# 8-dim attention heads: values and softmax denominators from one set of products, in a four-layer decoder on one core

## The chip, the cores and the metric

The program runs on one core of a Trainium2 chip. The metric is device time in microseconds of that core, lower is better. A core has five engines that run side by side, each with its own queue: PE (matrix products), DVE (vector work), ACT (pointwise functions), POOL (general vector work) and SP (which only starts transfers here). They are coupled by semaphores alone: an engine takes its instructions strictly in order and stops at a wait until another engine has signalled.

## The reference

A decoder of 32 sequences of 128 tokens, 128 features, passes through many layers. Four of them are attentions with 16 heads of 8 dimensions. All have this core (`_L0_attn_ref`):

```python
q = split_heads(x @ Wq + bq)          # 16 heads of 8
k = split_heads(x @ Wk + bk)
v = split_heads(x @ Wv + bv)
energy = jnp.einsum('bhqd,bhkd->bhqk', q, k)
energy = energy + bias[None]                              # L0_attn alone
att = jax.nn.softmax(energy / (scaling * temp), axis=-1)
out = jnp.einsum('bhqk,bhkd->bhqd', att, v)
out = out.transpose(0, 2, 1, 3).reshape(B, N, C)
return out @ Wp + bp
```

The second (the attention in `L1_ffn`) is causal, grouped in its keys and turned by rotary positions; the third (`L2_xattn`) takes keys and values from a context of 96 features and has a small two-layer projection behind it; the fourth (`L3_xattn`) takes keys and values from the context too. A residual and, but for the second, a layer norm follow.

## The kernel before

All four attentions are built by `attention8` (L682). It works on pairs of sequences: `n` counts the 32 sequences, `p = n // 2` the pairs, `s = n % 2` the half. The order of every engine is written out by hand in one loop over `n` per engine, and in it some steps stand only for even `n`, some only for odd ones.

For one sequence the softmax goes like this. PE forms rough scores of all heads in four PSUM banks (`score_roughly`, L1251, in two halves), DVE takes their row maxima (`maxima`, L1033, in two halves of 8 heads), PE turns the maxima (L1264), ACT copies them out (`evict_maxima`, L952), PE forms the exact scores with keys in the rows (L1271) and subtracts the maxima by a further product (L1279), and ACT takes the exponentials into `pT` (L966, L961 in `L0_attn`, again in two halves). Rough scores, exact scores and the next sequence's rough scores use the same four banks, so sequence after sequence goes through PE, DVE, PE and ACT in a ring. In `L0_attn` DVE adds the bias in between (`add_bias`, L1045), and there and in the causal layer PE adds bias or mask to the scores (L1233).

The rest hangs on the side of the ring. PE multiplies `pT` by the values, 16 products of 32 output rows each (`weigh`, L1293); `vz` holds the values with zeros around them so that the four heads of a 32-row group add up side by side. 16 further products by `ones4` sum `pT` over the keys, so that each of the 8 rows of a head holds its denominator (`add_up`, L1301). Both stand in one PSUM bank, `D`: columns 0 to 255 hold values of the pair, 256 to 511 denominators. In the trace every such product has two rows, so 16 of them read x32. When both sequences of pair `p-1` are in, DVE takes the reciprocal of the denominators (L1052) and multiplies (L1056) in `normalised(p-1)`, at even `n` behind the maxima; PE projects the result at odd `n` (`project_out`, L1324; with the hidden layer `hide`, L1312, and L1328), and DVE adds the residual (L1065).

```python
if n + 1 < NB:
    score_roughly(n + 1, [0])
if n >= 1:
    weigh(n - 1)
if n + 1 < NB:
    score_roughly(n + 1, [1])
if n >= 1:
    add_up(n - 1)
```

## Time and profile before

| | us |
|---|---|
| median of three runs | 3140.16 (3131.76 to 3142.49) |
| the profiled execution's own time | 3129.11 |
| its span, first to last instruction | 3127.3 |
| PE busy | 2682.1 (86%) |
| DVE busy | 1927.8 (62%) |
| ACT busy | 1380.7 (44%) |
| POOL busy | 1365.6 (44%) |

The stages run one after another. From the first to the last reading of rough scores (L1033) the four attentions stand at 16.5 to 247.3 us (`L0_attn`), 1255.6 to 1482.6 (`L1_ffn`), 1942.9 to 2148.6 (`L2_xattn`) and 2811.9 to 3001.1 (`L3_xattn`). Tile names in the profile leave the layer's number out: L_attn is `L0_attn` there, L_ffn the second, L_xattn the third and the fourth. A row of the timeline gives the start and the length of one or several merged instructions and, in brackets, how long the engine had stood idle before it and what ended that. PE durations run past the start of the next instruction, since products are pipelined; the time that one takes of the engine is the distance between starts.

### The profile page before, as it was taken

Reading aid. Unit: us, or ns where it says so; the run is one execution under the profiler, and the core shown is the slowest. Engines: PE = TensorE matmul, PEld = TensorE weight load, DVE = VectorE, ACT = ScalarE, POOL = GpSimd, SP = SyncE. Lnnn points to the kernel's source line nnn. Section 1 sums busy time; section 2 is a strip of 40 time slices with the busy share of each in tenths; the row PEclk is TensorE's granted clock in tenths of the full one; section 3 lists DMA queues with packets and bytes.
Section 4 is the critical chain, followed back from the end, with each engine's and each line's share of the span. In section 5 each row is a group of like instructions: output and inputs, shape, how many; then the busy total and the mean of one; then the engine's idle time right before and its main releaser. Section 6 shows DMA issues by size and latency. Waiting matters only on the chain. (4 is left out here: it accounts for less than half of the span.)

```text
span 3127.3 us, 78252 instructions
## 1 busy us (share of the span) xinstructions
PE 2682.1 (86%) x31745; PEld 1906.2 (61%) x31745; DVE 1927.8 (62%) x5040; ACT 1380.7 (44%) x3101; POOL 1365.6 (44%) x1474
## 2 busy tenths in 40 slices
PE   7894566666779997999999997998989999989986
PEld 4552333344446775565899985666367777765665
DVE  6888999355764444666544444564866666645665
ACT  4453555354445654444322223553144444435554
POOL 4773666173311222444233343553853333434556
PEclk9997777787889999999899997998999999999998
DMA  3000000400000001000000000001000000000000
GB/s 108 2 2 1 1 1 1 111 10 7 1 19 17 2 2 42 2 3 3 8 1 1 1 8 11 2 3 45 0 6 2 3 2 2 2 9 2 3 5 24
DMA packets 25796, 37.16 MB, mean 12 GB/s; under 512 B 760, under 2 KB 22656, under 8 KB 24576
## 3 DMA queue, kind: packets, MB, share of 16 engines
q1 hardware_dynamic: 25440, 32.16, 3.4%
q8 instruction: 255, 4.18, 0.6%
q14 instruction: 101, 0.83, 0.1%
HBM read 29.93 MB, written 2.23 MB: 10 GB/s over the span
## 5 line engine op out<-in xcount | busy, mean ns | idle before, releaser
L1501 POOL TENSOR_TENSOR L_attn__qk<-L_attn__turned 128x512 f32<-128x512 f32 x128 | 161.5, 1272 | 287.3 <-DVE L_attn__turned L1624 287.3
L4664 PE MATMUL psum<-L_ffn__e_hT,weights 128*128 128x256 f32 x1024 | 244.3, 382 | 0.0
L1033 DVE TENSOR_REDUCE L_xattn__nm<-psum 128x8 bf16<-128x1024 f32 x128 | 156.4, 1225 | 138.3 <-PE psum L1251 132.1
L1624 DVE TENSOR_TENSOR L_attn__turned<-psum,weights 128x1024 f32<-128x1024 f32 x128 | 153.4, 1219 | 94.0 <-PE psum L1737 89.2
L4664 PEld LDWEIGHTS psum<-L_ffn__e_hT,weights 128*128 128x128 f32 x1024 | 186.7, 192 | 20.2
L4511 DVE TENSOR_TENSOR L_ffn__e_a<-L_ffn__e_sg,psum 128x512 f32<-128x512 f32 x128 | 88.1, 688 | 176.0 <-ACT L_ffn__e_sg L4503 175.9
L4503 ACT ACTIVATE L_ffn__e_sg<-psum 128x512 f32<-128x512 f32 x128 | 76.4, 597 | 258.4 <-PE psum L4664 258.4
L966 ACT ACTIVATE L_xattn__pT<-psum 128x1024 f32<-128x1024 f32 x128 | 124.1, 1021 | 56.1 <-PE psum L1279 56.1
L1737 PE MATMUL psum<-L_attn__xT,weights 128*128 128x256 f32 x512 | 136.0, 399 | 3.9 <-DVE L_attn__turned L1624 3.2
L4677 PEld LDWEIGHTS psum<-weights,L_ffn__e_a 128*128 128x128 f32 x1024 | 134.4, 192 | 7.2 <-DVE L_ffn__e_a L4511 0.7
L4677 PE MATMUL psum<-weights,L_ffn__e_a 128*128 128x128 f32 x1024 | 135.1, 275 | 0.5 <-DVE L_ffn__e_a L4511 0.5
L4421 POOL TENSOR_TENSOR L_ffn__e_half<-L_ffn__e_prod 128x512 f32<-128x512 f32 x32 | 40.6, 1269 | 171.2 <-DVE L_ffn__e_prod L4520 171.2
L1552 ACT ACTIVATE L_attn__qk<-L_attn__qk 128x512 bf16<-128x512 f32 x128 | 77.2, 630 | 82.5 <-POOL L_attn__qk L1501 82.5
L1033 DVE TENSOR_REDUCE L_ffn__nm<-psum 128x8 bf16<-128x1024 f32 x64 | 78.2, 1225 | 55.4 <-PE psum L1251 55.4
L961 ACT ACTIVATE L_attn__pT<-L_attn__pT,L_attn__sc 128x1024 f32<-128x1024 f32 x64 | 73.0, 1149 | 76.3 <-DVE L_attn__pT L1045 76.3
L1737 PEld LDWEIGHTS psum<-L_attn__xT,weights 128*128 128x128 f32 x512 | 90.5, 192 | 25.6 <-issue 11.5
L3160 DVE MATCH_REPLACE8 L_xattn__front_left<-L_xattn__front_top,L_xattn__front_left 128x128 f32<-128x128 f32 x384 | 100.7, 273 | 0.0
L1033 DVE TENSOR_REDUCE L_attn__nm<-psum 128x8 bf16<-128x1024 f32 x64 | 78.0, 1221 | 24.8 <-PE psum L1251 24.8
L1633 DVE TENSOR_REDUCE L_attn__nm<-psum 128x8 bf16<-128x1024 f32 x64 | 75.4, 1220 | 26.4 <-PE psum L1770 25.8
L1972 POOL TENSOR_TENSOR L_xattn__rstd<-L_xattn__mv,eps 128x2 f32<-128x2 f32 x16 | 3.1, 195 | 198.3 <-DVE L_xattn__mv L2101 198.3
L1575 ACT ACTIVATE L_attn__pT<-psum 128x1024 f32<-128x1024 f32 x64 | 62.0, 1021 | 61.3 <-PE psum L1799 61.3
L3302 PE MATMUL psum<-L_xattn__front_diag,L_xattn__front_ex 128*128 128x128 f32 x256 | 53.5, 378 | 40.9 <-POOL L_xattn__front_ex L2989 39.4
(682 smaller groups left out, 7525.8 us busy)
## 6 DMA issues: line engine op xcount, KB each, us to landing
L_xattn__conv_toeplitz<-s4d_kernel SPq DMA_DIRECT2D x5, 1024.0 KB, 10.9
weights<-pack SPq DMA_DIRECT2D x1, 3328.0 KB, 12.6
weights<-pack SPq DMA_DIRECT2D x1, 3140.0 KB, 10.0
weights<-s4d_kernel SPq DMA_DIRECT2D x3, 1024.0 KB, 9.1
L_attn__bias_tables<-pack SPq DMA_DIRECT2D x1, 2048.0 KB, 9.9
out_dram<-X SPq DMA_DIRECT2D x8, 256.0 KB, 2.3
weights<-pack SPq DMA_DIRECT2D x1, 1603.5 KB, 15.0
ctxT<-ctxT_in SPq DMA_DIRECT2D x1, 1536.0 KB, 12.0
```

The source lines that it names most:

```text
L966: nc.scalar.activation(unit, scores[u], ACT.Exp, scale=scale).then_inc(p_sb, 1)
L1033: nc.vector.tensor_reduce(nm[:, n % 2, :].rearrange("p (g c) -> p g c", g=4)[:, 2 * u:2 * u + 2, 0:4], scores[u].rearrange("p g (i q) -> p ...
L1501: nc.gpsimd.tensor_tensor(qk[:, p % 2, u], turned[:, g % 2, :, 0:2 * P], turned[:, g % 2, :, 2 * P:4 * P], ALU.add).then_inc(qk_sb, 1)
L1552: nc.scalar.activation(qk16[:, p % 2, u], qk[:, p % 2, u], ACT.Copy).then_inc(qk16_sb, 1)
L1624: nc.vector.tensor_tensor(turned[:, g % 2], proj[u % 2].unsqueeze(1).to_broadcast([P, 2, 4 * P]), k.w(name + "rope").rearrange("p (t q) -> ...
L1633: nc.vector.tensor_reduce(nm[:, n % 2, :].rearrange("p (g c) -> p g c", g=4)[:, 2 * u:2 * u + 2, 0:4], scores[u].rearrange("p g (j q) -> p ...
L1737: last = nc.tensor.matmul(proj[place % 2][:, 2 * P * t:2 * P * t + 2 * P], w[:, P * c:P * c + P], xT[:, p % 2, :], start=True, stop=True)
L3160: last = nc.vector.match_replace(left[:, u % 2, j, h, :], top[:, u % 2, j, h, 8 * r:8 * r + 8], source(u, r, j, h), 2 * NEG)
L4503: nc.scalar.activation(sg[:, g % 2, :], gate[g % 2], ACT.Silu).then_inc(sg_sb, 1)
L4511: nc.vector.tensor_tensor(a[:, g % 2].rearrange("p c s q -> p (c s q)"), sg[:, g % 2, :], up[g % 2], ALU.mult).then_inc(a_sb, 1)
L4664: last = nc.tensor.matmul(bank[g % 2][:, 256 * c:256 * c + 256], k.w(name + w)[:, o:o + P], hT, start=True, stop=True)
L4677: last = nc.tensor.matmul(Y[s][e // 4][:, P * (e % 4):P * (e % 4) + P], a[:, g % 2, c, s, :], k.w(name + "Wd")[:, P * (2 * e + c):P * (2 * ...
```

## The change

The zeros of `vz` beside each head's values become ones in 8 columns. The weights of one product are then, for a head, 8 columns of values and 8 of ones (even heads) or ones and values (odd heads), with zeros in the other 16. One set of 16 products gives values and denominators: the bank `D` holds even heads in columns 0 to 255 and odd heads in columns 256 to 511, and in each the values of a head in its own 8 rows and its denominators in the 8 rows of its neighbour (or the other way round). `add_up` goes.

To get them in place, ACT scales the even-head half by two 0/1 masks (`own_half`: the values that stand right, and the denominators), DVE adds the odd-head half with the opposite masks (`both_halves`, two instructions), so `both[:, 0]` holds all values and `both[:, 1]` all denominators, the latter in their neighbour's rows. DVE takes the reciprocal of these, PE exchanges neighbouring groups of 8 rows by a permutation matrix (`swap`, two products of 128x128x128), and DVE multiplies (`normalised`). These steps are put at fixed places of each engine's loop, and PE's `project_v`, `project_out` and `weigh` change places with the rough scores.

```diff
-        vz = sb("vz", [P, 2, 2, 4, 4, 40])
+        vz = sb("vz", [P, 4, 4 * P + 2 * D8])
+        own, both = sb("own", [P, 2, 2 * P]), sb("both", [P, 2, 2 * P])
...
-                nc.gpsimd.memset(vz[:], 0.0).then_inc(zeroed, 1)
+                for kind in range(2):
+                    heads = vz[:, :, 2 * P * kind:2 * P * kind + 2 * P].rearrange("p a (m c) -> p a m c", c=4 * D8)
+                    nc.gpsimd.memset(heads[:, :, :, D8 - D8 * kind:2 * D8 - D8 * kind], 1.0)
+                    last = nc.gpsimd.memset(heads[:, :, :, 2 * D8:4 * D8], 0.0)
+                last.then_inc(zeroed, 1)
...
+                def own_half(p):
+                    act.wait_ge(pv_ps, 2 * p + 2)
...
+                    if p >= 1:
+                        act.wait_ge(both_sb, p)
+                    for kind in range(2):
+                        last = nc.scalar.activation(own[:, kind, :], D[:, 0:2 * P], ACT.Identity,
+                                                    scale=halves_of_16[:, kind:kind + 1])
+                    last.then_inc(own_sb, 1)
...
                         if p < LAST:
                             evict_v(p + 1)
+                        if p >= 1:
+                            own_half(p - 1)
...
+                def both_halves(p):
+                    dve.wait_ge(own_sb, p + 1)
...
+                    for kind in range(2):
+                        last = nc.vector.scalar_tensor_tensor(
+                            out=both[:, kind, :], in0=D[:, 2 * P:4 * P], scalar=halves_of_16[:, 1 - kind:2 - kind],
+                            in1=own[:, kind, :], op0=ALU.mult, op1=ALU.add)
+                    last.then_inc(both_sb, 1)
+                    dve.wait_ge(both_sb, p + 1)
+                    if p >= 1:
+                        dve.wait_ge(rd_ps, p)
+                    nc.vector.reciprocal(rd[:], both[:, 1, :]).then_inc(rd_sb, 1)
+
                 def normalised(p):
-                    dve.wait_ge(pv_ps, 2 * p + 2)
-                    nc.vector.reciprocal(rd[:], D[:, 2 * P:4 * P]).then_inc(rd_sb, 1)
-                    dve.wait_ge(rd_sb, p + 1)
+                    dve.wait_ge(rd_ps, p + 1)
                     if p >= 2:
                         dve.wait_ge((hid_ps if mlp else y_ps), p - 1)
-                    nc.vector.tensor_tensor(oT[:, p % 2, :], D[:, 0:2 * P], rd[:], ALU.mult).then_inc(o_sb, 1)
+                    nc.vector.tensor_tensor(oT[:, p % 2, :].rearrange("p (s q) -> p s q", s=2),
+                                            D[:].rearrange("p (s e q) -> p s e q", s=2, e=2)[:, :, 1, :],
+                                            both[:, 0, :].rearrange("p (s q) -> p s q", s=2),
+                                            ALU.mult).then_inc(o_sb, 1)
...
+                    if n % 2 == 1 and p >= 1:
+                        normalised(p - 1)
                     if n + 1 < NB:
                         maxima(n + 1)
...
                         if p >= 1:
-                            normalised(p - 1)
+                            both_halves(p - 1)
...
-                    if s == 0 and p >= 1:
-                        pe.wait_ge(o_sb, p)
...
+                    if p >= 1:
+                        pe.wait_ge(o_sb if s == 1 else both_sb, p)
+                    for kind in range(2):
+                        for i in range(2):
+                            for g in range(4):
+                                m = 2 * g + i
+                                o = 2 * P * kind + 4 * D8 * m - 2 * D8 * i
+                                last = nc.tensor.matmul(
+                                    D[32 * g:32 * g + 32, 2 * P * kind + P * s:2 * P * kind + P * s + P],
+                                    vz[:, p % 2 * 2 + s, o:o + 4 * D8], pT[:, n % 2, 2 * m + kind, :], start=i == 0,
+                                    stop=i == 1, skip_group_check=True)
                     last.then_inc(pv_ps, 1)
+
+                def swap(p):
+                    pe.wait_ge(rd_sb, p + 1)
+                    for s in range(2):
+                        last = nc.tensor.matmul(D[:, 2 * P * s + P:2 * P * s + 2 * P], k.w("swap8"),
+                                                rd[:, P * s:P * s + P], start=True, stop=True, skip_group_check=True)
+                    last.then_inc(rd_ps, 1)
...
                     score(n, turned)
+                    if n % 2 == 1 and p >= 1:
+                        swap(p - 1)
```

PE's queue, one odd `n` of `L3_xattn`, before (L1186 turns the next x, L1251 are rough scores, L1301 is `add_up`):

```order
L1279 MATMUL psum<-L_xattn__nmT,sel 128x128 x16
L1186 MATMUL psum<-const,X 128x128 x2
L1324 MATMUL psum<-weights,L_xattn__oT 128x128 x2
L1251 MATMUL psum<-L_xattn__k16m,L_xattn__q 128x512 x2
L1293 MATMUL psum<-L_xattn__pT,L_xattn__vz 32x128 x16
L1251 MATMUL psum<-L_xattn__k16m,L_xattn__q 128x512 x2
L1301 MATMUL psum<-L_xattn__pT,const 32x128 x16
L1264 MATMUL psum<-ident_bf,L_xattn__nm 64x128 x2
```

The same stretch of PE's queue in the changed kernel (L1348 is `swap`, L1295 rough scores, L1370 the projection, L1339 `weigh`):

```order
L1323 MATMUL psum<-L_xattn__nmT,sel 128x128 x16
L1348 MATMUL psum<-L_xattn__rd,const 128x128 x2
L1230 MATMUL psum<-const,X 128x128 x2
L1295 MATMUL psum<-L_xattn__k16m,L_xattn__q 128x512 x2
L1370 MATMUL psum<-weights,L_xattn__oT 128x128 x2
L1295 MATMUL psum<-L_xattn__k16m,L_xattn__q 128x512 x2
L1339 MATMUL psum<-L_xattn__pT,L_xattn__vz 32x128 x16
L1308 MATMUL psum<-ident_bf,L_xattn__nm 64x128 x2
```

The exchange stands directly behind the exact scores and ahead of both halves of the next rough scores; `add_up` is gone, and `weigh` stands behind the second half.

DVE's queue over one pair of `L3_xattn` before, beginning at even `n`:

```order
L1033 TENSOR_REDUCE L_xattn__nm<-psum 128x2x4 x2
L1052 RECIPROCAL L_xattn__rd<-psum 128x256
L1056 TENSOR_TENSOR L_xattn__oT<-psum,L_xattn__rd 128x256
L1033 TENSOR_REDUCE L_xattn__nm<-psum 128x2x4 x2
L1065 TENSOR_TENSOR L_xattn__res<-psum,L_xattn__xb 128x256
L1071 BN_STATS L_xattn__st<-L_xattn__res 128x6 x2
L1074 BN_AGGR L_xattn__mv<-L_xattn__st 128x2 x2
```

And in the changed kernel:

```order
L1056 TENSOR_REDUCE L_xattn__nm<-psum 128x2x4 x2
L1081 SCALAR_TENSOR_TENSOR L_xattn__both<-psum,const,L_xattn__own 128x256 x2
L1088 RECIPROCAL L_xattn__rd<-L_xattn__both 128x256
L1094 TENSOR_TENSOR L_xattn__oT<-psum,L_xattn__both 128x256
L1056 TENSOR_REDUCE L_xattn__nm<-psum 128x2x4 x2
L1106 TENSOR_TENSOR L_xattn__res<-psum,L_xattn__xb 128x256
L1112 BN_STATS L_xattn__st<-L_xattn__res 128x6 x2
L1115 BN_AGGR L_xattn__mv<-L_xattn__st 128x2 x2
```

Two instructions come ahead of the reciprocal, and the multiplication behind it now waits for PE's exchange before the next maxima can be taken.

## Rows read from the trace of the kernel before

**Rows 1.** Busy time by engine over the four attentions' stretches, summed

```profile
sum 884.00, PE 823.02 PEld 515.42 DVE 600.77 ACT 442.01 POOL 471.02; mean PE 205.76 PEld 128.86 DVE 150.19 ACT 110.50 POOL 117.75
```

**Rows 2.** Busy time of line L1301 (add_up) over the four stretches

```profile
sum 896.00, PE 141.12; mean PE 35.28
```

**Rows 3.** Timeline of PE in L3_xattn: start, length, what, idle before

```profile
2927.65 0.61 PE L1225 MATMUL psum<-weights,ctxT 96*128 96x128 f32 x4
2928.19 0.39 PE L1251 MATMUL psum<-L_xattn__k16m,L_xattn__q 32*128 32x512 bf16 x2
...
2929.84 1.08 PE L1301 MATMUL psum<-L_xattn__pT,const 128*32 128x128 f32 x32
2930.85 0.62 PE L1264 MATMUL psum<-ident_bf,L_xattn__nm 128*64 128x128 bf16 x2
...
2933.45 0.68 PE L1324 MATMUL psum<-weights,L_xattn__oT 128*128 128x128 f32 x4 [0.30 <-DVE L_xattn__oT L1056]
```

**Rows 4.** Timeline of ACT in L3_xattn

```profile
2920.89 1.94 ACT L966 ACTIVATE L_xattn__pT<-psum 128x1024 f32<-128x1024 f32 x2 [0.86 <-PE psum L1279]
...
2926.76 1.94 ACT L966 ACTIVATE L_xattn__pT<-psum 128x1024 f32<-128x1024 f32 x2 [1.01 <-PE psum L1279]
2928.59 0.48 ACT L917 ACTIVATE L_xattn__kT<-psum,weights 128x256 f32<-128x256 f32 x1
...
2931.05 0.45 ACT L933 ACTIVATE L_xattn__vz<-psum 128x128 f32<-128x128 f32 x2 [1.25 <-PE psum L1301]
...
2932.80 1.94 ACT L966 ACTIVATE L_xattn__pT<-psum 128x1024 f32<-128x1024 f32 x2 [0.86 <-PE psum L1279]
```

**Rows 5.** Timeline of DVE in L3_xattn

```profile
2928.62 2.56 DVE L1033 TENSOR_REDUCE L_xattn__nm<-psum 128x8 bf16<-128x1024 f32 x2 [2.40 <-PE psum L1251]
2931.09 1.75 DVE L1052 RECIPROCAL L_xattn__rd<-psum 128x256 f32<-128x256 f32 x1
2932.88 0.42 DVE L1056 TENSOR_TENSOR L_xattn__oT<-psum,L_xattn__rd 128x256 f32<-128x256 f32 x1
```

**Rows 6.** Groups by line and form: count, busy us, mean ns of one

```profile
L4003 DVE SCALAR_TENSOR_TENSOR L_ffn__npre<-psum,weights,L_ffn__rh 128x256 f32<-128x256 f32 x8 | 3.9, 484 | 0.3
L4013 DVE SCALAR_TENSOR_TENSOR L_ffn__hnew<-L_ffn__zd,L_ffn__nt 128x256 f32<-128x256 f32 x8 | 8.1, 1014 | 0.3
```

**Rows 7.** Timeline of one pair of L0_attn: DVE's bias additions, ACT's exponentials

```profile
156.21 2.36 DVE L1045 TENSOR_TENSOR L_attn__pT<-psum,L_attn__bias_tables 128x1024 f32<-128x1024 f32 x2 [0.55 <-PE psum L1279]
157.46 2.28 ACT L961 ACTIVATE L_attn__pT<-L_attn__pT,L_attn__sc 128x1024 f32<-128x1024 f32 x2 [2.27 <-DVE L_attn__pT L1045]
...
163.33 2.35 DVE L1045 TENSOR_TENSOR L_attn__pT<-psum,L_attn__bias_tables 128x1024 f32<-128x1024 f32 x2
...
169.97 1.23 DVE L1045 TENSOR_TENSOR L_attn__pT<-psum,L_attn__bias_tables 128x1024 f32<-128x1024 f32 x1 [0.55 <-PE psum L1279]
```

**Rows 8.** PE's waits in L0_attn, 16 to 256 us: total, times, longest

```profile
PE psum L1233 <- POOL L_attn__k16m L780: 12.0, 8, 3.4
```

**Rows 9.** Timeline of ACT: L1_ffn one pair apart, L2_xattn by sequences

```profile
1399.66 1.94 ACT L966 ACTIVATE L_ffn__pT<-psum 128x1024 f32<-128x1024 f32 x2 [1.32 <-PE psum L1279]
...
1414.17 1.94 ACT L966 ACTIVATE L_ffn__pT<-psum 128x1024 f32<-128x1024 f32 x2 [1.32 <-PE psum L1279]
...
2060.88 1.94 ACT L966 ACTIVATE L_xattn__pT<-psum 128x1024 f32<-128x1024 f32 x2 [0.86 <-PE psum L1279]
...
2067.82 1.94 ACT L966 ACTIVATE L_xattn__pT<-psum 128x1024 f32<-128x1024 f32 x2 [0.72 <-PE psum L1279]
...
2073.85 1.94 ACT L966 ACTIVATE L_xattn__pT<-psum 128x1024 f32<-128x1024 f32 x2 [0.86 <-PE psum L1279]
```

**Rows 10.** PE in L0_attn after a wait; PE busy and granted clock by microsecond

```profile
121.56 0.41 PE L1233 MATMUL psum<-L_attn__bias,ident_bf 32*32 32x512 bf16 x8 [1.75 <-POOL L_attn__k16m L780]
...
123.00:124.00 1.00, 1.00 (x25) 0.50 0.00 0
```

**Rows 11.** Timeline of DVE at the start of L2_xattn

```profile
1935.26 2.56 DVE L1111 COPY L_xattn__bvw<-weights 128x128 f32<-128x128 f32 x1
```

More of the change, by code:

```diff
@@ L127, in host_pack @@
     put("const", "sel4", (inside % 32 == np.arange(4)[None, :]).astype(np.float32))
-    put("const", "ones4", rows(np.repeat(np.eye(4), D8, 1).reshape(-1)).astype(np.float32))
+    odd = np.arange(P) // D8 % 2
+    put("const", "swap8", np.eye(P, dtype=np.float32)[np.arange(P) ^ D8])
+    put("const", "halves", np.stack([1 - odd, odd], 1).astype(np.float32))
     put("later", "iota8", rows(np.tile(np.arange(NE, dtype=np.float32), NB)))
@@ L1016, in _ @@
                             hidden(p - 1)
+                own_half(LAST)
                 if mlp:
@@ L1162, in late_dve @@
                 def late_dve(dve):
+                    both_halves(LAST)
                     normalised(LAST)
@@ L1406, in _ @@
                     if n >= 1:
-                        add_up(n - 1)
+                        weigh(n - 1)
                     if mlp and n % 2 == 1 and p >= 1:
@@ L1410, in _ @@
                 weigh(NB - 1)
-                add_up(NB - 1)
                 def late_pe(pe):
+                    swap(LAST)
                     if mlp:
```

44 lines of the change are left out of this document (20 added, 24 removed).

## The prediction

> **What bounds the kernel now.** I read the busy times of the four attentions' stretches first. PE is busy for 823.02 of 884 us there, DVE for 600.77, ACT for 442.01 [rows 1]: PE looks like the bound. Then the timeline of one pair of sequences in `L3_xattn`, engine by engine, because a busy PE can also be a PE that fills a ring of waits. The ring can be read off: ACT begins the exponentials of the even sequence at 2926.76 (call it A), PE's rough scores start at 2928.19, DVE reads the maxima from 2928.62 to 2931.18, and ACT's next exponentials begin at 2932.80, 1.62 us behind the maxima (turn, exact scores, subtraction) [rows 3 to 5]. Of PE's work only this is in the ring. Rough scores could start when the first half of the exponentials is through, about A+1.1 (two halves take 1.94, the first a little over half of it), yet start at A+1.43, since PE has the projections in front. So the ring alone needs 1.1 + 0.43 + 2.56 + 1.62 = 5.71 us a sequence, and the pair takes 2932.80 - 2920.89 = 11.91, or 5.95 each [rows 4]. PE can give back 0.5 us a pair here, whatever is taken from it. `L1_ffn` has 14.51 a pair and `L2_xattn` 12.97 (6.94 + 6.03) [rows 9]; there PE's queue itself is long. `L0_attn` has 13.76, 7.12 for the even sequence and 6.64 for the odd [rows 7], and DVE's bias additions are in its ring.
>
> **What goes.** `add_up`: 141.12 us of PE [rows 2], 1.01 per sequence (2929.84 to 2930.85 [rows 3]), 2.02 per pair.
>
> **What comes, per pair.** PE: four rows of 128x128x128, as `project_v` has them, 2927.65 to 2928.19, so 0.54 [rows 3]. ACT: two instructions of 256 columns with an operand per partition, 0.48 each as the eviction of keys has it [rows 4], 0.85 to 0.96 together; I take 0.9. DVE: two instructions that combine a PSUM half, a mask and an SBUF half. The nearest row, with the same kinds of operands, has 484 ns; one with both tensors in SBUF has 1014, so two cost between 0.97 and 2.03, and I take 0.95, the low end, as they overlap a little [rows 6]. The reciprocal reads SBUF now. No row has that at 256 columns: it lies between a plain pass of these columns (0.42) and what it takes from PSUM (1.75) [rows 5]; I take 1.75, since the multiplication, a plain pass that reads the same bank, shows that the length is not in the reading of PSUM. POOL's four smaller fills in place of one are off any path, between nothing and a few us in all.
>
> **Where it stands, in L3_xattn.** At even n: second rough half at A+2.04, `weigh` through at A+3.45. ACT takes the values of the next pair (0.45 [rows 4]) and then `own_half`, until A+4.75. DVE has the maxima by A+4.09 and must wait 0.66, then adds halves to A+5.70 and has the reciprocal at A+7.50. The next exponentials start at A' = A+5.71 (before: 2932.80 - 2926.76 = 6.04). So far 0.3 gained. But at odd n PE's queue has `swap` directly behind the exact scores, and it waits for a reciprocal that ends at A'+1.79. Behind it in the queue stand the turn of x and the rough scores, for which DVE, and so the ring, waits. Swap ends at A+8.09, the turn (half of the four rows, 0.27) at A+8.36, the maxima start 0.43 later at A+8.79 (DVE's multiplication fits in between), end at A+11.35, and the following exponentials start at A+12.97. The pair goes from 11.91 to 12.97: **+1.06**, for 15 pairs +16 us. Before, the reciprocal ran beside the exact scores and only the projection waited for it, 0.30 [rows 3].
>
> **L2_xattn.** By PE's queue: 12.97 less 2.02, plus 0.54, plus the wait of 1.8, plus 0.7 at even n, where PE's 6.03 - 1.01 = 5.02 falls under the ring's 5.71, less some 0.2 of the old wait: 13.8, **+0.8**, in all +12.
>
> **L1_ffn.** PE's queue is fuller, its mask products lengthen both the ring and the way to the reciprocal: 14.51 - 2.02 + 0.54 + 1.8 = 14.8, **+0.3**, in all +5.
>
> **L0_attn.** Let B be the start of the bias addition, 156.21. The exponentials take B+1.25 to B+3.53, the three evictions of keys and queries about 1.2 and that of values 0.4, to B+5.15, `own_half` to B+6.0. DVE, which has its maxima by about B+4.7 (2.3 for the bias and 2.4 for the maxima behind it), waits for it, adds the halves (B+6.95), and the reciprocal ends at B+8.75. The next bias addition is queued behind it: it starts at B+8.8 instead of B+7.12. At odd n: bias addition 2.26, multiplication to 2.65, projection (0.15 + 0.54) and the second rough half with its bias products (0.7), second maxima 4.15 to 5.4, 1.6 more for the exact scores: 7.0 instead of 6.64. Pair **+2.05**, in all +31. Some of it falls into PE's 12.0 us of waits for POOL's masks [rows 8], which POOL's own work sets; I take 7 off: +24.
>
> **The ends.** Behind the last `weigh` the three new steps lengthen the way to the last projection by about 2.5, one or two sums less shorten it by 1 to 2: +0.7 in each of four stages, +3.
>
> **The clock.** After a wait of 1.75 us the granted clock was 0.50 (1.2 GHz) in the microsecond from 123 on [rows 10]. The new wait of 1.8 is as long, 60 times. Between no fall and a fall each time, at about 1 us of the ring's products each, lie 0 and 60 us; I take 7.
>
> **Sum.** 24 + 5 + 12 + 16 + 3 + 7 = +67. The profiled execution took 3129.11 (span 3127.3 and 1.8 around it); changed, 3196. The median of the runs lies 11.05 above the profiled one, so I forecast 3140.16 + 67 = **3207** for the median, 2.1% slower.
>
> **A rule on the shared port.** A DVE copy of 128 columns took 2.56 us at 1935.26, twice as long per instruction as a reading of 1024 columns (1.28) [rows 11, 5]. The Trainium skill, page "SBUF — State Buffer", section "Who interferes with whom", says that a DVE instruction with at most one SBUF input and outside the two-port modes does not contend with GpSimd, and that copies and casts can enter those modes. By that, the combining instructions keep 484 ns beside POOL. It does not list the reciprocal; if it were held like the copy, the second rival would follow.
>
> **Rivals.**
> 1. *The clock falls at most of the new waits.* For it: 1.75 us sufficed once. Against: of the shorter waits, as that of 0.30 [rows 3], none shows such a mark, and a stretch of 1.8 us is as long as one that did it, not longer. Price: 45 falls or more at 1 to 2 us instead of 7, 60 to 110 us more: about 3285. Chance 0.10.
> 2. *The reciprocal from SBUF is held by POOL's work*, as the copy was, by 0.9 to 1.9 us, directly on the way to the swap: 62 times 0.9, about +56: 3263. Against it: unless it runs in a mode that takes two ports, its single source should leave POOL alone, and its length in columns points to its arithmetic. Chance 0.07.
> 3. *The reciprocal from SBUF is short*, and the kernel gets faster: the point from which it decides is a reciprocal ready before about A'+0.5, so 1.3 less than 1.75. At 0.42 the swap waits 0.46 only. Pairs come to 11.6, 12.6, 13.5 and 14.4 in the order L3, L2, L1, L0: -0.3, -0.4, -1.0 and +0.6, times 15 about -16: 3121 with the ends. For it speaks only that no row shows this form; against, that nothing in the trace makes reading PSUM cost 1.3 us. Together with other ways in which PE's 107 us less could show after all (141.12 less 34 for swaps): chance 0.09.
> 4. *No difference*: the waits take back just what PE gives, if own_half and swap are ready 0.5 to 0.8 earlier than I have them, for which ACT would have to take the halves ahead of the values. The queue speaks against it. 3140. Chance 0.07.
>
> That the change doesn't do what it says is no case here: 16 products of 32 rows are gone from the queue.
>
> **How the numbers follow.** The forecast (3150 to 3260) has 0.67. Slower by over 0.3% (9 us, about what a measurement of this kernel tells from no change) holds the forecast, rivals 1 and 2 and a little of 4: 0.85. Within 0.3%: 0.06. Faster: 0.09. The range, 3150 to 3275, leaves out rival 3, most of 4 and the upper part of rival 1. Its lower end has the clock at nothing and L0_attn's and L2_xattn's excess halved, its upper end two combining instructions at 2.03 (62 times 1.06, +65).
>
> **What would show it.** In the changed trace: `add_up` gone and PE busy down by about 100 us in the four stretches; PE idle before `swap`, released by DVE's reciprocal, 1 to 2 us each, 60 to 64 times, 90 to 120 us in all; pairs of 13.0, 13.8, 14.8 and 15.8 us; in `L0_attn` DVE idle before `both_halves`, released by ACT. Wrong would be the forecast if `swap` is found waiting under 0.5 us; if the reciprocal is not 1.75 us; if PE's idle time is released by anything but the reciprocal; or if the stages keep their pairs and the loss stands in the clock.

## The result, and the profile after

| | before | changed |
|---|---|---|
| median of the runs | 3137.1 (3131.76 to 3142.49, 4 runs) | 3273.5 (3273.27 to 3279.48, 4 runs) |
| span of the profiled execution | 3127.3 | 3271.4 |
| granted clock, mean over the span | 0.914 | 0.874 |
| PE busy | 2682.1 | 2733.8 |

The ratio is 1.0433 (95% interval 1.0414 to 1.0452): slower by 136 us, where 67 were forecast. The span grew by 144.1 us. From the first to the last reading of rough scores the four attentions now stand at 17.9 to 278.5, 1299.6 to 1535.5, 1998.5 to 2243.2 and 2911.8 to 3135.0 us, so they grew by 29.8, 8.9, 39.0 and 34.0, in all 111.7. The rest, 32.4, lies outside these stretches.

The four stretches by busy time and granted clock (PEclk), first of the kernel before, then of the changed one; rows in the order L0_attn, L1_ffn, L2_xattn, L3_xattn:

```profile
16.00:247.00 231.00, 203.26 (x3530) 121.67 (x3528) 190.29 (x223) 118.60 (x218) 151.95 (x197) 0.96 0.07 20
1256.00:1483.00 227.00, 223.95 (x4101) 136.00 (x4100) 147.27 (x179) 94.66 (x220) 105.17 (x100) 0.99 0.01 3
1943.00:2149.00 206.00, 194.42 (x3154) 127.08 (x3158) 123.48 (x171) 114.99 (x246) 103.56 (x105) 0.96 0.01 2
2812.00:3001.00 189.00, 174.57 (x3025) 112.06 (x3025) 120.59 (x161) 102.15 (x213) 104.19 (x107) 0.96 0.02 5
```

```profile
18.00:279.00 261.00, 221.07 (x2652) 121.62 (x2648) 201.87 (x252) 127.13 (x246) 152.35 (x197) 0.81 0.05 15
1300.00:1536.00 236.00, 208.91 (x3203) 117.54 (x3202) 167.50 (x207) 104.68 (x248) 105.40 (x101) 0.98 0.01 2
1998.00:2243.00 245.00, 206.46 (x2242) 126.18 (x2242) 135.09 (x198) 128.14 (x274) 103.68 (x105) 0.83 0.01 1
2912.00:3135.00 223.00, 184.39 (x2122) 110.68 (x2126) 132.49 (x190) 113.85 (x241) 104.58 (x107) 0.82 0.01 3
```

The first number after the comma is PE's busy time, with its instructions. In L3_xattn some 900 rows of products fewer (450 products) keep PE busy 10 us longer. The clock column says why: 0.96 became 0.81 to 0.83 in three of the four stretches. In L1_ffn it stayed, and there PE's busy time fell by 15 us.

The waits of PE for the reciprocal (total, number, longest), in place of the 0.30 of [rows 3]:

```profile
PE psum L1348 <- DVE L_xattn__rd L1088: 60.9, 32, 3.7
PE psum L1348 <- DVE L_attn__rd L1088: 31.7, 16, 3.7
PE psum L1348 <- DVE L_ffn__rd L1088: 29.2, 16, 3.8
```

121.8 us in 64 waits, 1.9 each; the longest, of 3.7 and 3.8, are the last one of each attention. The groups of the new steps in the third and fourth attention (busy us, mean ns of one, then idle time before them), which answer to [rows 2, 5, 6]:

```profile
L1339 PE MATMUL psum<-L_xattn__pT,L_xattn__vz 128*32 128x128 f32 x2048 | 92.2, 338 | 0.0
...
L1088 DVE RECIPROCAL L_xattn__rd<-L_xattn__both 128x256 f32<-128x256 f32 x32 | 56.1, 1753 | 1.1
...
L1081 DVE SCALAR_TENSOR_TENSOR L_xattn__both<-psum,const,L_xattn__own 128x256 f32<-128x256 f32 x64 | 28.0, 480 | 32.4 <-ACT L_xattn__own L954 32.4
L954 ACT ACTIVATE L_xattn__own<-psum,const 128x256 f32<-128x256 f32 x64 | 27.0, 482 | 14.0 <-PE psum L1339 14.0
```

The reciprocal from SBUF has 1753 ns against 1749 from PSUM, the combining instruction 480, `own_half` 482. The weighing is the same instruction as before, with 338 ns instead of the 280 it had in the kernel before; in L1_ffn, where the clock stayed, it has 279.

Two pairs of L3_xattn on PE, after [rows 3]: the first at full clock, the second with a fall:

```profile
3025.70 0.71 PE L1348 MATMUL psum<-L_xattn__rd,const 128*128 128x128 f32 x4 [1.87 <-DVE L_xattn__rd L1088]
...
3026.56 0.39 PE L1295 MATMUL psum<-L_xattn__k16m,L_xattn__q 32*128 32x512 bf16 x2
...
3038.55 1.22 PE L1348 MATMUL psum<-L_xattn__rd,const 128*128 128x128 f32 x4 [1.87 <-DVE L_xattn__rd L1088]
...
3040.13 0.61 PE L1295 MATMUL psum<-L_xattn__k16m,L_xattn__q 32*128 32x512 bf16 x2
```

The wait is 1.87 us both times. The swap takes 0.71 the first time and 1.22 the second. The first pair is the exception. Of the 14 such waits inside each of L0_attn, L2_xattn and L3_xattn, 14, 14 and 13 had a fall of the clock during them or behind them; of the 14 of 1.73 us in L1_ffn it was three. In all the granted clock fell 47 times in the four stretches, 14, 3, 15 and 15 times in their order, against 6 times in the kernel before. The microseconds around the second (the last three numbers are granted clock, DMA share, GB/s): half speed, 1.2 GHz, begins while the wait is still on.

```profile
3037.00:3038.00 1.00, 0.00 (x0) 0.00 (x0) 1.00 (x1) 1.00 (x2) 0.57 (x1) 1.00 0.00 0
3038.00:3039.00 1.00, 0.45 (x2) 0.45 (x3) 0.49 (x1) 0.47 (x1) 0.00 (x0) 0.73 0.00 0
3039.00:3040.00 1.00, 1.00 (x6) 0.80 (x5) 0.19 (x1) 0.00 (x0) 0.00 (x0) 0.50 0.00 0
```

ACT's exponentials of the same pairs, after [rows 4]:

```profile
3023.68 1.94 ACT L986 ACTIVATE L_xattn__pT<-psum 128x1024 f32<-128x1024 f32 x2 [0.30 <-PE psum L1323]
3030.96 1.94 ACT L986 ACTIVATE L_xattn__pT<-psum 128x1024 f32<-128x1024 f32 x2 [1.01 <-PE psum L1323]
3036.53 1.94 ACT L986 ACTIVATE L_xattn__pT<-psum 128x1024 f32<-128x1024 f32 x2 [0.30 <-PE psum L1323]
3046.25 1.94 ACT L986 ACTIVATE L_xattn__pT<-psum 128x1024 f32<-128x1024 f32 x2 [1.10 <-PE psum L1323]
```

The odd sequence takes 7.28 us at full clock and 9.72 with a fall; the even one 5.57. So the pair has 12.85 (forecast 12.97, before 11.91) and this fall adds 2.44.

DVE in L0_attn, with ACT's exponentials of two pairs apart, after [rows 7]:

```profile
144.47 0.88 DVE L1081 SCALAR_TENSOR_TENSOR L_attn__both<-psum,const,L_attn__own 128x256 f32<-128x256 f32 x2 [1.20 <-ACT L_attn__own L954]
145.38 1.75 DVE L1088 RECIPROCAL L_attn__rd<-L_attn__both 128x256 f32<-128x256 f32 x1
147.05 2.29 DVE L1068 TENSOR_TENSOR L_attn__pT<-psum,L_attn__bias_tables 128x1024 f32<-128x1024 f32 x2
```

```profile
139.86 2.28 ACT L981 ACTIVATE L_attn__pT<-L_attn__pT,L_attn__sc 128x1024 f32<-128x1024 f32 x2 [1.98 <-DVE L_attn__pT L1068]
...
155.76 2.28 ACT L981 ACTIVATE L_attn__pT<-L_attn__pT,L_attn__sc 128x1024 f32<-128x1024 f32 x2 [2.27 <-DVE L_attn__pT L1068]
```

DVE stands idle 1.20 us for `own_half`, and the bias addition starts only behind the reciprocal. This pair takes 15.90 with a fall in it. L1_ffn has pairs of 15.15 at full clock (forecast 14.8), and L2_xattn this one of 16.86, again with a fall, after [rows 9]:

```profile
1400.45 1.94 ACT L986 ACTIVATE L_ffn__pT<-psum 128x1024 f32<-128x1024 f32 x2 [0.60 <-PE psum L1323]
...
1415.60 1.94 ACT L986 ACTIVATE L_ffn__pT<-psum 128x1024 f32<-128x1024 f32 x2 [0.60 <-PE psum L1323]
```

```profile
2104.67 1.94 ACT L986 ACTIVATE L_xattn__pT<-psum 128x1024 f32<-128x1024 f32 x2 [0.30 <-PE psum L1323]
...
2121.53 1.02 ACT L986 ACTIVATE L_xattn__pT<-psum 128x1024 f32<-128x1024 f32 x1 [0.30 <-PE psum L1323]
```

And an end, that of L3_xattn, from the last exponentials to the last residual, before and changed:

```profile
3003.94 1.94 ACT L966 ACTIVATE L_xattn__pT<-psum 128x1024 f32<-128x1024 f32 x2 [1.01 <-PE psum L1279]
...
3012.12 0.42 DVE L1065 TENSOR_TENSOR L_xattn__res<-psum,L_xattn__xb 128x256 f32<-128x256 f32 x1 [0.27 <-PE psum L1324]
```

```profile
3139.52 1.94 ACT L986 ACTIVATE L_xattn__pT<-psum 128x1024 f32<-128x1024 f32 x2 [1.36 <-PE psum L1323]
...
3153.56 0.42 DVE L1106 TENSOR_TENSOR L_xattn__res<-psum,L_xattn__xb 128x256 f32<-128x256 f32 x1 [0.78 <-PE psum L1370]
```

8.18 us before, 14.04 now. In L0_attn, L1_ffn and L2_xattn the same distance grew from 7.58 to 12.99, from 7.82 to 11.96 and from 14.04 to 18.16. The four ends are 19.5 us longer in all.

### The profile page after: what moved, and what is told of

The parts are those of the page before. It is cut to its first block and busy times, and to the rows that moved or that the text cites. A ratio compares the mean times of both kernels' runs of the same rounds, so it can differ in the third digit from the quotient of the medians.

```text
span 3271.4 us, 71022 instructions
## 1 busy us (share of the span) xinstructions
PE 2733.8 (84%) x27905; PEld 1901.7 (58%) x27905; DVE 1989.3 (61%) x5168; ACT 1431.2 (44%) x3229; POOL 1363.4 (42%) x1486
## 5 line engine op out<-in xcount | busy, mean ns | idle before, releaser
L1672 DVE TENSOR_TENSOR L_attn__turned<-psum,weights 128x1024 f32<-128x1024 f32 x128 | 153.4, 1219 | 94.1 <-PE psum L1785 89.2
L1339 PE MATMUL psum<-L_xattn__pT,L_xattn__vz 128*32 128x128 f32 x2048 | 92.2, 338 | 0.0
```

What stands on the lines that cost most here:

```text
L1339: last = nc.tensor.matmul(D[32 * g:32 * g + 32, 2 * P * kind + P * s:2 * P * kind + P * s + P], vz[:, p % 2 * 2 + s, o:o + 4 * D8], pT[:, ...
L1672: nc.vector.tensor_tensor(turned[:, g % 2], proj[u % 2].unsqueeze(1).to_broadcast([P, 2, 4 * P]), k.w(name + "rope").rearrange("p (t q) -> ...
```

## The experiments

All medians are of four or more runs, and each ratio is to runs of the kernel before on the same chip, whose median was 3131.0 to 3137.1. The table gives, for each profiled execution, the length from first to last maxima of the four attentions and the granted clock in them; the sections say what each run was for.

| | median, us | ratio to before (95%) | L0 | L1 | L2 | L3 | clock L0, L1, L2, L3 |
|---|---|---|---|---|---|---|---|
| before | 3137.1 | | 230.8 | 227.0 | 205.7 | 189.2 | .96 .99 .96 .96 |
| changed | 3273.5 | 1.0433 (1.0414–1.0452) | 260.6 | 235.9 | 244.7 | 223.2 | .81 .98 .83 .82 |
| e1 | 3212.1 | 1.0256 (1.0229–1.0283) | 238.4 | 240.2 | 223.1 | 208.8 | 1.0 .99 .96 .96 |
| e8 | 3198.5 | 1.0189 (1.0164–1.0214) | 244.6 | 234.0 | 219.0 | 204.0 | .95 .98 .95 .95 |
| e3 | 3122.2 | 0.9970 (0.9953–0.9987) | 234.1 | 215.6 | 200.4 | 183.7 | .93 .98 .94 .96 |
| e4 | 3134.1 | 1.0001 (0.9985–1.0017) | 232.0 | 223.2 | 198.9 | 191.7 | .95 .98 .94 .96 |
| e5 | 3166.5 | 1.0100 (1.0078–1.0121) | 258.0 | 226.7 | 206.2 | 191.7 | .89 .99 .96 .96 |
| e6 | 3261.2 | 1.0387 (1.0350–1.0425) | 255.5 | 245.2 | 241.1 | 213.5 | .91 .98 .91 .97 |
| e10b | 3261.5 | 1.0409 (1.0389–1.0429) | 269.1 | 245.4 | 230.8 | 219.7 | .85 .97 .90 .91 |
| e9b | 3389.8 | 1.0817 (1.0794–1.0840) | 289.4 | 262.3 | 265.8 | 260.8 | .82 .97 .87 .79 |
| e12 | 3223.5 | 1.0272 (1.0251–1.0294) | 264.7 | 221.5 | 220.5 | 215.5 | .82 .99 .94 .87 |
| e2 | 3163.9 | 1.0089 (1.0067–1.0112) | 269.5 | 212.0 | 197.3 | 183.2 | .82 1.0 .96 .94 |
| e7 | 3110.4 | 0.9920 (0.9902–0.9937) | 210.2 | 214.8 | 198.1 | 184.7 | .94 .98 .95 .93 |
| e11b | 3112.5 | 0.9929 (0.9905–0.9953) | 206.2 | 213.9 | 202.8 | 184.9 | 1.0 1.0 .95 .95 |

### The wait kept, the clock held: e1_filled and e8_filled_7

```diff
 def swap(p):
+    pe.wait_ge(both_sb, p + 1)
+    for _ in range(10):                 # 7 in e8_filled_7
+        nc.tensor.matmul(D[:, P:2 * P], k.w("swap8"), ident, start=True, stop=True, ...)
     pe.wait_ge(rd_sb, p + 1)
```

> The changed kernel, with ten products of 128x128x128 whose result nobody reads put on PE between the end of the combining additions and the swap, about 1.35 us at full clock, inside the reciprocal's 1.75 us. The order and every wait of the other engines stay. Theory (half of the loss is the clock: PE's idle 1.9 us before the swap brings the granted clock down from 0.96 to 0.82 in three of the four attentions): the clock there goes back to 0.93 or more, the stretches from first to last maxima shrink by 12 to 20 us each in L0_attn, L2_xattn and L3_xattn, nothing in L1_ffn, and the kernel takes 3210 to 3235 instead of 3273. Rival A (the ring alone: the swap's wait delays the rough scores, and the clock is only seen beside it): time unchanged, 3265 to 3280, even with a higher clock. Rival B (the clock falls for another reason than this idle time): clock stays at 0.82 and the fillers cost, above 3290.

> As e1_filled with seven fillers instead of ten. There the ten took 2.34 us and ended 0.6 us after the reciprocal, so they held the swap up; seven take 1.64 us and end inside the 1.75. Theory (the fillers keep the clock, and what is left is the ring of waits at full clock): pairs 0.6 us shorter than in e1_filled, L3_xattn 12.7 us, 3175 to 3190, clock 0.91 to 0.92. Rival (the idle time of some 0.2 us before and after is again enough for falls): clock under 0.90, 3200 or more. Rival (the fillers of e1_filled cost nothing): 3205 to 3215.

Measured: 3212.1 and 3198.5. The stretches of e8_filled_7 sum to 901.6 us against 964.4 of the changed kernel and 852.7 before. Nothing but the fillers differs, the clock falls 6 times instead of 47, and in L3_xattn 11 of the 15 distances from one pair to the next are 12.85 us:

```profile
2996.34 1.94 ACT L986 ACTIVATE L_xattn__pT<-psum 128x1024 f32<-128x1024 f32 x2 [0.30 <-PE psum L1323]
...
3009.19 1.94 ACT L986 ACTIVATE L_xattn__pT<-psum 128x1024 f32<-128x1024 f32 x2 [0.30 <-PE psum L1323]
...
3022.04 1.94 ACT L986 ACTIVATE L_xattn__pT<-psum 128x1024 f32<-128x1024 f32 x2 [0.30 <-PE psum L1323]
```

```profile
3009.42 1.83 PE L1348 MATMUL psum<-const 128*128 128x128 f32 x14
3011.20 0.71 PE L1352 MATMUL psum<-L_xattn__rd,const 128*128 128x128 f32 x4
```

So 62.8 us of the loss in the stretches is the clock, and 48.9 is the ring of waits at the clock of before. (The profiled execution of e8 lies 8 us above its median, so the clock's share may be a little larger.) Of the expectations, that for ten fillers held in time, though L0_attn and L2_xattn shrank by more than it said (22.2 and 21.6 us), L1_ffn grew by 4.3, and 1.35 us for ten products was wrong: I had taken the duration of one row for that of a product, which has two. The ten take 2.34, so they held the swap up by 0.6. With seven the median is 8 us or more above what was expected: L0_attn had falls again (0.95), and L3_xattn won 4.8 us where 9 were expected.

### The reciprocal made short: e3_undivided

```diff
-nc.vector.reciprocal(rd[:], both[:, 1, :]).then_inc(rd_sb, 1)
+nc.vector.tensor_tensor(rd[:], D[:, 2 * P:4 * P], both[:, 1, :], ALU.mult).then_inc(rd_sb, 1)
```

> The changed kernel with the reciprocal replaced by a multiplication of PSUM by SBUF over the same 256 columns, so the division is left out; order, swap and all waits stay. It takes 0.42 instead of 1.75 us. Theory (the length of the reciprocal is what PE's queue waits for): the swap waits 0.4 to 0.6 us, no fall of the clock follows it, the kernel takes 3110 to 3135. Rival A (the order itself, with the longer chain own half, combining, swap, costs, whatever the reciprocal takes): 3170 or more. Rival B (the clock falls because PE has 100 us less work in the same time): clock near 0.85 in the attentions although the waits are short, 3160 to 3200.

Measured: 3122.2, and the waits for it 37.5 us in 61, 0.6 each. All the new steps and their order stand, PE has as few products as in the changed kernel, and this one is 151 us faster than the changed one and a little faster than before. Both rivals fall: neither the order nor the lighter PE costs anything on the whole as long as the wait is short (L0_attn stays 3.3 us above before, the other three lie below). This run also takes 1.33 us a pair off DVE; how much such a load costs apart from its place is seen in e5 below. The third rival of the prediction had put such a kernel at 3121.

### What PE's sums were worth: e4_no_sums

```diff
 if n >= 1:
     weigh(n - 1)
 if n + 1 < NB:
     score_roughly(n + 1, [1])
-if n >= 1:
-    add_up(n - 1)
```

> The kernel before the change without its 16 products by ones per sequence, so the denominators are left out (the reciprocal is taken of the values instead); nothing is added or moved. It tells what PE's 141 us alone are worth. Theory (ring of 5.71 us a sequence): pairs shorten by 0.5 us in L3, 1.5 in L2, 2.0 in L1 and nothing in L0, 60 us in all: 3070 to 3090, and the clock stays where it was. Rival A (PE bounds all four stretches): 120 to 140 us less, 3000 to 3020. Rival B (less work on PE lowers the clock and gives the time back): about 3137, clock in the attentions below 0.9.

Measured: 3134.1, ratio 1.0001. All three expectations fall (the third had the time right, but not the clock, which is 0.94 or more). 141 us of PE's work are worth nothing, with the clock nearly unchanged. L3_xattn's pairs were 6.03 + 5.87 = 11.90 us, as before the change: the sums stood where PE waited for the maxima anyway. PE's 823 busy us of 884 [rows 1] were no bound in any of the stretches but L2_xattn and L1_ffn, and there by 7 and 4 us in all.

### The wait alone, in the kernel before: e5_load_behind and e6_load_ahead

```diff
 nc.vector.reciprocal(rd[:], D[:, 2 * P:4 * P]).then_inc(rd_sb, 1)
 dve.wait_ge(rd_sb, p + 1)
+nc.vector.reciprocal(unread, ident twice)       # e6_load_ahead
 nc.vector.tensor_tensor(oT[:, p % 2, :], D[:, 0:2 * P], rd[:], ALU.mult).then_inc(o_sb, 1)
+nc.vector.reciprocal(unread, ident twice)       # e5_load_behind
```

> The kernel before the change, with one more reciprocal of 256 columns (1.75 us) on DVE per pair of sequences, behind the multiplication, whose result nobody reads. PE waits for nothing new. It is the pure load, so that the next run's wait can be told from it. Expected: nothing in L3_xattn, L2_xattn and L1_ffn or under 0.5 us a pair (DVE is idle 1.2 to 2.4 us before the maxima), and up to 1.75 us a pair in L0_attn, where DVE is near full: 3140 to 3165, granted clock 0.90 to 0.92. If DVE's load is what costs in the changed kernel (rival), this is 3190 or more.

> The kernel before the change, with the same additional reciprocal ahead of the multiplication, so that the output projection, which stands in PE's queue ahead of the rough scores, waits 1.75 us longer (about 2.0 instead of 0.3 us in L3_xattn). All 16 products by ones stay in place. Theory (a wait of about 2 us in PE's queue ahead of the rough scores is the whole loss, first in the ring and then in the clock): pairs longer by 1 to 1.8 us at full clock, the granted clock in L0_attn, L2_xattn and L3_xattn falls to 0.80 to 0.88, time 3220 to 3290. Rival A (the clock falls in the changed kernel because PE has less to do there): the clock stays above 0.90 here and the time is 3190 to 3215. Rival B (the load alone): as the run beside it.

Measured: 3166.5 and 3261.2. Behind the multiplication the load costs 27.1 us in L0_attn, 1.7 a pair, and at most 2.5 elsewhere. Ahead of it, PE waits 118.5 us in 64 waits for `oT`:

```profile
3033.25 0.68 PE L1327 MATMUL psum<-weights,L_xattn__oT 128*128 128x128 f32 x4 [1.91 <-DVE L_xattn__oT L1059]
```

So of this run's 124 us, 95 come from the place alone: a wait of 1.9 us in PE's queue ahead of the rough scores rebuilds most of the changed kernel's loss in the old one. But the clock did not do what was expected of it: 0.97 in L3_xattn, 0.91 in L0_attn and L2_xattn, with 25 falls in the four stretches instead of 47. With all its products in place, PE kept its clock better behind a wait of the same length.

### Is it the lighter PE? e9b_weighed_twice and e10b_no_sums_ahead

```diff
-for kind in range(2):                    # weigh, e9b_weighed_twice
+for kind in (0, 1, 0, 1):
```

> The changed kernel with its 16 weighing products per sequence issued twice, the second time over the first, with the same result. That gives PE back the 16 products that the change took away, at the same place behind the second rough half, where it had room; the swap's wait for the reciprocal stays at 1.9 us. Theory formed from the runs so far (a wait of 1.9 us lowers the clock only where PE is also lightly used between the waits; the removed products are what kept it up): granted clock of L3_xattn and L2_xattn back to 0.90 to 0.97, L0_attn 0.88 or more, 3190 to 3235. Rival (the wait alone lowers the clock): 0.82 in these stages as in the changed kernel, 3275 to 3310.

> The run e6_load_ahead (kernel before, the additional reciprocal ahead of the multiplication, so that PE waits 1.9 us for it) without the 16 products by ones; the denominators are left out. Against e4_no_sums it adds only the wait, against e6_load_ahead it takes away 141 us of PE's work. Theory (wait and light use together lower the clock): clock 0.80 to 0.86 in L0_attn, L2_xattn and L3_xattn, and the kernel is slower than e6_load_ahead with all its products (3261), 3265 to 3330. Rival (the wait alone; less work can only help): clock as in e6_load_ahead, 0.91 or more, 3240 to 3260.

Measured: 3389.8 and 3261.5. The second goes halfway: without the sums the clock is lower (0.91 instead of 0.97 in L3_xattn, 0.85 instead of 0.91 in L0_attn), and PE's 141 us less bring no time, 3261.5 against 3261.2. The first contradicts the theory: as many products as before, and the clock was 0.79 in L3_xattn (0.82 in the changed kernel) and only 0.87 in L2_xattn (0.83). Nor did the doubled products stand where PE had room: in L1_ffn, where the clock stayed, a pair took 16.89 us instead of 15.15. So this run changes the length of the pair with the amount of work, and the two are not told apart. In L3_xattn many pairs in a row were 17.0 to 17.1 us long, with the swap at half speed each time (1.22 us instead of 0.71):

```profile
3090.41 1.22 PE L1348 MATMUL psum<-L_xattn__rd,const 128*128 128x128 f32 x4 [1.87 <-DVE L_xattn__rd L1088]
3107.45 1.23 PE L1348 MATMUL psum<-L_xattn__rd,const 128*128 128x128 f32 x4 [1.87 <-DVE L_xattn__rd L1088]
```

So the amount of PE's work between the waits does not by itself settle whether one of them brings the clock down. My theory from the first eight runs fell.

### The turn ahead of the swap: e12_turn_first

```diff
 score(n, turned)
-if n % 2 == 1 and p >= 1:
-    swap(p - 1)
 ...                                      # turn(p + 2), project_k_turned(p + 2)
+if n % 2 == 1 and p >= 1:
+    swap(p - 1)
 if n + 1 < NB:
     score_roughly(n + 1, [0])
```

> The changed kernel with one step moved: the turn of x (and in L1_ffn the turned projection of keys) stands ahead of the swap in PE's queue instead of behind it. The wait for the reciprocal gets shorter by the turn, 0.3 us (1.87 to about 1.55 us in L3_xattn), and less work stands between the wait and the rough scores. At an unchanged clock this gives 0.3 us a pair, 60 times, less what the ring covers: about 3255 (changed: 3273). Theory A (whether a wait brings the clock down depends on a few tenths of its length and on what stands beside it): granted clock of L3_xattn and L2_xattn back above 0.90, time 3180 to 3230. Theory B (each wait over about 1.5 us does it in these stages): clock stays 0.80 to 0.85, time 3245 to 3265. If nothing moves (3268 to 3280), the swap's place behind the turn is not in the ring at all.

Measured: 3223.5, 50 us less than changed for one step moved. The waits are 94.1 us in 64, 1.5 each. L2_xattn's clock is back at 0.94 and that stretch 24.2 us shorter, L1_ffn is 14.4 shorter, L3_xattn 7.6 with 0.87, and L0_attn is 4.0 longer with 0.82. At full clock the pairs of L2_xattn and L3_xattn hardly changed (13.86 and 12.79 us, against 13.86 and 12.85 in e8), so there the gain is the clock's: 2 and 10 falls instead of 15 and 15. In L1_ffn the ring itself got shorter, 14.28 instead of 15.15. Theory A holds in L2_xattn, theory B in L0_attn; the time lies with A. One step of a few tenths of a microsecond decides, but not alike in all stages.

### Out of the ring: e2_late, e7_spread, e11b_v_first

e2_late puts the swap behind the rough scores:

```diff
 score(n, turned)
-if n % 2 == 1 and p >= 1:
-    swap(p - 1)
 ...
     if n % 2 == 1 and p >= 1:
-        project_out(p - 1, ...)
+        project_out(p - 2, ...)          # from p >= 2; residual and norm too
 ...
 weigh(n - 1)
+if n % 2 == 1 and p >= 1:
+    swap(p - 1)
```

```diff
-normalised(p - 1)                        # DVE, odd n
 maxima(n + 1)
+normalised(p - 1)
```

> The changed kernel with the same arithmetic, but the swap behind the next rough scores and the weighing in PE's queue, the multiplication behind the maxima in DVE's, and projection, residual and norm a whole pair of sequences later, so that nothing of the ring stands behind the wait for the reciprocal. Theory (the loss is that one wait, in the ring and in the clock): PE waits for the reciprocal under 0.3 us, the clock in the attentions goes back to about 0.95, pairs of 11.6 (L3), 12.2 (L2), 13.2 (L1) and 14.6 us (L0): the kernel takes 3080 to 3125, faster than before the change (3137). Rival A (the extra work on DVE and ACT, with the wait for own_half, is the loss): 3200 or more, with DVE the releaser of most of the idle time. Rival B (only the ring is mended, the clock stays low since PE simply has less to do): 3140 to 3180 with a clock of 0.85.

Measured: 3163.9, outside the theory's range and by its number in rival B's, but not with rival B's clock (0.94 to 1.0 in three stages). PE's waits for the reciprocal are gone in the loop, and L1_ffn, L2_xattn and L3_xattn came out at 212.0, 197.3 and 183.2, below before (15.0, 8.3 and 6.0 us). L0_attn got worse instead, 269.5 at a clock of 0.82: there DVE's reciprocal still stood ahead of the bias addition, and POOL came late with its masks, so PE had other waits in its place (at L0_attn's bias products 31.9 us for DVE in 27 waits, the longest 3.1, and 17.1 for POOL in 5, the longest 4.8).

e7_spread mends that. POOL makes its masks before norm and bias, and in L0_attn the reciprocal goes behind the maxima of the odd sequence:

```diff
 maxima(n + 1)                            # DVE, L0_attn
 even n: both_halves(p - 1)
-        reciprocal(p - 1)
+odd n:  reciprocal(p - 1)
+        # swap on PE at the next even n behind the exact scores,
+        # multiplication on DVE there ahead of the maxima
```

> A version meant to beat both: as e2_late in L1_ffn, L2_xattn and L3_xattn; POOL's norm and bias stand behind the masks at even n, so that its masks no longer wait for the residual; in L0_attn the reciprocal stands behind the maxima at odd n, the swap one sequence later behind the exact scores, the multiplication ahead of the maxima and the moments at even n, so that DVE does them where it was idle. Theory: L0_attn goes from e2_late's 269.6 us (first to last maxima) to 225 to 238, the others keep 212, 197 and 183, the clock in L0_attn is above 0.93: 3115 to 3135, a little faster than before (3136). Rival (L0_attn is held by POOL's masks and DVE's bias additions whatever the order): 3150 to 3165.

Measured: 3110.4, ratio 0.9920 (0.9902 to 0.9937): faster than both kernels, and a little better than expected, since L0_attn took 210.2 us, 20.6 less than before the change. Its pairs have 13.15 us:

```profile
153.88 2.28 ACT L989 ACTIVATE L_attn__pT<-L_attn__pT,L_attn__sc 128x1024 f32<-128x1024 f32 x2 [1.66 <-DVE L_attn__pT L1078]
...
157.20 1.74 DVE L1100 RECIPROCAL L_attn__rd<-L_attn__both 128x256 f32<-128x256 f32 x1
...
167.03 2.28 ACT L989 ACTIVATE L_attn__pT<-L_attn__pT,L_attn__sc 128x1024 f32<-128x1024 f32 x2 [1.66 <-DVE L_attn__pT L1078]
```

How much of L0_attn's gain is in POOL's order and how much in DVE's was not taken apart; nor was it tried whether the kernel before would win as much by the same two moves.

e11b_v_first is e7_spread with `project_v(p + 1)` ahead of `score_roughly(n + 1, [0])` again:

> The run e7_spread with the projection of the values back ahead of the first rough half, as in the kernel before. It tells what the change's other reordering gives back. Theory (PE's projections stand in the ring at even n): pairs longer by 0.45 us in L3_xattn and L2_xattn, about 0 to 0.5 in L1_ffn and nothing in L0_attn, where DVE's bias additions cover it: 3122 to 3135. Rival (the values' projection is hidden wherever it stands): 3107 to 3114, as e7_spread.

Measured: 3112.5, like e7_spread's 3110.4 within the intervals. The rival held by its number, but not by its reason. ACT's exponentials one pair apart in L3_xattn, first of e7_spread, then of e11b_v_first:

```profile
2849.40 1.94 ACT L994 ACTIVATE L_xattn__pT<-psum 128x1024 f32<-128x1024 f32 x2 [0.83 <-PE psum L1355]
...
2860.75 1.94 ACT L994 ACTIVATE L_xattn__pT<-psum 128x1024 f32<-128x1024 f32 x2 [0.83 <-PE psum L1355]
```

```profile
2847.58 1.94 ACT L994 ACTIVATE L_xattn__pT<-psum 128x1024 f32<-128x1024 f32 x2 [0.61 <-PE psum L1355]
...
2859.08 1.94 ACT L994 ACTIVATE L_xattn__pT<-psum 128x1024 f32<-128x1024 f32 x2 [0.61 <-PE psum L1355]
```

With the projection ahead of the rough half a pair takes 11.50 instead of 11.35 us here, 12.81 instead of 12.55 in L2_xattn and 13.87 instead of 13.74 in L1_ffn, so the projection is hidden only in part (0.45 was expected in the first two). In the profiled executions L0_attn makes up for it: 206.2 us without a fall of the clock, against 210.2 with three in e7_spread.

## Why the prediction was right and where it was not

**The mechanism was right.** The swap waits in PE's queue for the reciprocal, 1.9 us, 64 times (forecast 1 to 2 us, 60 to 64 times, 90 to 120 in all; 121.8). e3 takes the length out of the wait and the loss is gone; e6 puts the wait into the kernel before, and costs 95 us more than e5, which has the same load in another place, of the 136 to be explained. In L0_attn DVE waits for `own_half`, as said.

**The durations were right.** Reciprocal from SBUF 1753 ns (1750 taken), combining 0.88 (0.95), `own_half` 0.84 to 0.87 (0.9), swap 0.54 by the starts (3025.70 to 3026.24). The second rival falls: the reciprocal kept its 1753 ns in all 64 cases, in 56 of them beside work of POOL. The 1014 ns of [rows 6], from which the upper end of the range was taken, is the mean of two different durations: five instructions of 1366 to 1370 ns beside a POOL addition and three of 424 and 425 with POOL idle. On the combining instructions the trace agrees with what the Trainium skill says on the page "SBUF — State Buffer", "Who interferes with whom": they kept 473 to 485 ns, 109 of the 128 beside work of POOL.

**The four terms at full clock were right in sum.** Of e8, whose clock is that of before but for 0.02 at most, most pairs have 15.44, 15.15, 13.86 and 12.85 us from L0_attn to L3_xattn, forecast 15.8, 14.8, 13.8 and 13.0. By the stretches: L0_attn +13.7 (forecast +24), L1_ffn +7.0 (+5), L2_xattn +13.3 (+12), L3_xattn +14.8 (+16): 48.9 against 57. L0_attn was put too high, in its pairs (+1.68 at full clock instead of +2.05) and in what falls into its old waits for POOL, which came to 12 us and of which 7 were taken off.

**The clock was mis-sized: 7 taken, 62.8 measured** in the four stretches (964.4 less e8's 901.6). The step that failed is "between no fall and a fall each time lie 0 and 60 us; I take 7": the changed kernel has 47 falls in the stretches and e8 has 6, and both the number and the price were too low. The one fall priced above cost 2.44 us; 62.8 us over 41 falls are 1.5 each (an estimate), where 1 was taken. The first rival, "45 falls or more at 1 to 2 us", at 3285 with a chance of 0.10, described the kernel better than the forecast did, in number and price; only L1_ffn, with three falls behind 14 waits, stands apart from it. The trace of before held more on this than [rows 10], outside the attentions: seven waits of 2.22 us at L2816 (864 to 938 us), each with a fall, and four of 1.88 to 1.98 at L4177 (787 to 811), one with a fall. One of each kind, with the microsecond behind it (the granted clock is the third number from the right):

```profile
890.02 0.51 PE L2816 MATMUL psum<-L_attn__pkv,L_attn__phi 32*128 32x136 f32 x8 [2.22 <-DVE L_attn__kvz L2727]
891.00:892.00 1.00, 1.00 (x7) 0.50 0.00 0
...
803.00 0.71 PE L4177 MATMUL psum<-L_ffn__wvo,L_ffn__hnew 128*128 128x128 f32 x4 [1.98 <-DVE L_ffn__hnew L4013]
804.00:805.00 1.00, 0.98 (x14) 1.00 0.00 0
```

By these rows a fall behind most of the new waits was not a rival with a chance of 0.10.

**The ends were mis-sized: 3 taken, 19.5 measured** (7.58, 7.82, 14.04 and 8.18 us before; 12.99, 11.96, 18.16 and 14.04 changed). In part this is the clock, which was down there too: in e8 the end of L3_xattn took 11.86 (3075.15 to 3087.01). That is still 3.7 more than before in place of 0.7, so the fewer sums shortened it by little or nothing.

**That the time lies in the range is luck.** 3273.5 is 1.5 us below the upper end of 3275. That end was reached with combining instructions of 1014 ns, and they have 480; clock and ends together came out 72 us above their terms, which on top of 3207 would be outside the range, and L0_attn 10 us below its own. One sign did not come true either: PE's busy time in the four stretches was to fall by about 100 us and rose from 796 to 821, since each product took longer at the lower clock.

**One argument was false without harm.** "PE can give back 0.5 us a pair": e4 took all 141 us of the sums away and L3_xattn's pairs stayed at 11.90. The even sequence did get shorter in the changed kernel, 5.57. By e4 this is not the missing sums; that it is the projection that moved is likely (in e11b its place is worth 0.15 us a pair) but not shown.

**What stays open.** 111.7 (stretches) and 19.5 (ends) leave 13 of the span's 144. From the last maxima of L0_attn to the first of L1_ffn it took 1021.1 us instead of 1008.3, of which 5.4 are the end of L0_attn; e4, in which nothing between the attentions differs from before, had 1016.0, so part is scatter between executions. And it is open what makes a wait of 1.9 us bring the clock down in one stage and not in the next: e6, e9b, e10b and e12 rule out the length of the wait alone and PE's load alone. What the traces show is that falls come in series (in e9b pair after pair), that the pair's length at full clock differs from run to run as well as the number of falls, and that 0.3 us moved from behind the wait to before it ended the series in L2_xattn. No run changed the pair's length alone.

## What to carry to other kernels

Ask of every engine that is called the bound what the step removed from it was hiding behind: here 141 us of a PE that was 93% busy were worth nothing, and the change that took them away, by the wait that came with it, cost 136. In a queue that runs in order, a step that waits for another engine belongs behind the work on which the ring depends, with what follows from it one turn later: that, with the steps of DVE and POOL moved alike in L0_attn, turned the same arithmetic from 4.3% slower to 0.8% faster. And where a change brings in a new gap on PE, look through the whole trace, outside the changed stage too, for gaps of that length: where most of them have a fall of the clock behind them, price a fall at each new one, and take the no-fall case as the rival.
